# A decoder stack on one core: other PSUM banks for the attention layers, and masks ahead of the query projection

## The chip, the cores and the metric

The kernel runs on one core of one Trainium2 chip. The core has five engines that run side by side and meet through semaphores: TensorE (PE: matrix products and transposes, which write into PSUM), VectorE (DVE), ScalarE (ACT), GpSimd (POOL) and SyncE (SP, here for DMA). PSUM has 8 banks of 128 partitions by 512 fp32 values. Each engine takes its own instructions strictly in the order written; an instruction that waits holds up all behind it on the same engine. The metric is the device time of one execution in microseconds (us).

## The reference

Twelve layers of a decoder (four blocks of self attention, cross attention and feed forward) work on x of 8 sequences x 128 positions x 128 values, each as `x = x + layer(layernorm(x))`. Five of the twelve are attentions with 16 heads of 8 values: L0x (cross, rotary), L1a (self, causal), L1x (cross, with a distance bias), L2x (cross, with a mask), L3a (self, rotary, causal). L1x stands for them:

```
x = x + _L1_xattn_ref(_layernorm(x), ctx_1024, Wq, bq, Wkv, bkv, Wo, bo)

q = query @ Wq + bq
k, v = jnp.split(kv @ Wkv + bkv, 2, axis=-1)      # 16 heads of 8
scores = jnp.einsum('bhqd,bhkd->bhqk', q, k) * scale + bias[None]
attn = jax.nn.softmax(scores, axis=-1)
out = jnp.einsum('bhqk,bhkd->bhqd', attn, v)
return out @ Wo + bo
```

## The kernel before

**Two groups, woven.** The 8 sequences are two groups g = 0, 1 of four. For every engine one Python generator per group writes the instructions; each `yield n, phase` gives the layer's number and a phase, and `weave` (L83) always lets the generator with the smaller pair go on, group 0 where they are equal. So the order on every engine is fixed when the kernel is built, and the phases alone set it.

**Banks.** `bank(i)` of group g is PSUM bank 4g + i. In an attention layer the key projection goes to `bank(1)`, the value projection to `bank(2)`, the transposed layer norm to `bank(3)`, the query projection to `bank(0)` (in L0x and L3a banks 0 and 1 hold the rows first and later their transposes). ACT reads them into SBUF as `QT`, `KT` and `vaug` (L915 or L913, L865 or L823, L834); in L1x and L2x DVE writes `vaug` and adds its bias (L1148).

**Units.** A unit u is one half (8 heads) of one sequence's heads; a group has 8 units. Its scores take two banks. Three pairs of banks, `PAIRS` (L177), go round between the groups: unit u of group g uses pair (2u + g) mod 3. Banks 6 and 7 hold the weighted values of group 0 and 1. For a unit PE writes the mask into the two banks (`biased`, L441: an identity times a bf16 mask, one matmul a bank, in L1x three), adds the scores on top (`scores`, L453: two matmuls over 32 partitions), DVE takes the maximum (L1155) and subtracts it into SBUF (L1161), PE transposes the eight heads back into the same two banks (`turned`, L466, its instructions at L469), ACT takes the exponential (L843), and PE multiplies with the values (`weighted`, L472). POOL spreads the keys of one sequence over heads (`KTm`, L333; the first of L0x, L1a and L3a is DVE's, L1143).

**The opening.** `attend` of PE (L439) first waits, for both groups, for QT, KT and vaug, since unit 0 of group 0 lies in banks 4 and 5 and unit 0 of group 1 in banks 2 and 3. Then PE's order is: mask and scores of unit 0 of group 0, the same of group 1, transposes of unit 0 of group 0, mask and scores of its unit 1, and so on. In L1x and L2x the keys and values of both groups are projected at phase 0, xn is transposed at phase 2, q projected at phase 4, and `attend` begins at phase 20. In L1a q, k and v are projected at phase 4; in L0x and L3a queries and keys are rotated on DVE and POOL and transposed at phase 8.

**The end.** `out_proj` (L514) turns the result in `bank(2)` and projects it into `bank(0)`. As these belong to pairs in turn, it waits for the last exponential but one of group 1 (group 0) or for the last result of group 0 (group 1).

Of the kernel before, what the change touches and what calls it, by code (L numbers as in the profile page):

```python
# [14 lines left out]
P = 128  # L15
B = 8
GB = 4
GROUPS = B // GB
W4 = GB * P
H = 16  # L20
HD = P // H
HG = 4
# [69 lines left out]
def build(nc, x_d, ctx_d, mask_d, w_d, r_d, c_d, k_d, b_d, out_d, marks):  # L92
# [81 lines left out]
        return bank  # L174

    all_banks = ps[:, :].rearrange("p (b c) -> p b c", c=512)
    PAIRS = (all_banks[:, 4:6, :], all_banks[:, 2:4, :], all_banks[:, 0:2, :])  # L177

    def pair(g, u):

# [221 lines left out]
    def _(pe):  # L402
        def mm(out, lhsT, rhs, start=True, stop=True, **k):
            return pe.matmul(out, lhsT, rhs, start=start, stop=stop, **k)  # L404
# [11 lines left out]
        def program(g):  # L416
# [22 lines left out]
            def attend(n, l):  # L439

                def biased(u, i):  # L441

                    r, out = 2 * (u % 2) + i, pair(g, u)[:, i, :]
                    if l == "L1x":
                        odd = out.rearrange("p (j k) -> p j k", j=HG)[:, 1::2, :]
                        mm(out, identb, alibi0[:, HG * r:HG * r + HG, :], stop=False)
                        mm(odd, identb, alibi1[:, 2 * r:2 * r + 2, :], start=False, stop=False)
                        mm(odd, identb, alibi2[:, 2 * r:2 * r + 2, :], start=False, stop=False)
                    else:
                        mask = t.dmask[:, u // 2, :] if l == "L2x" else causalb  # L450
                        mm(out, identb, mask.unsqueeze(1).to_broadcast([P, HG, P]), stop=False)

                def scores(u):  # L453
                    b, half = divmod(u, 2)
                    if 2 * u + g >= 3:
                        pe.wait_ge(*s.at(f"{l}.exp{(2 * u + g - 3) // 2}", 1 - g))
                    for i in range(2):
                        biased(u, i)
                    if half == 0:
                        pe.wait_ge(*s.at(f"{l}.keys{b}"))  # L460
                    for i in range(2):
                        r = 32 * (2 * half + i)
                        ins = mm(pair(g, u)[:, i, :], QT[r:r + 32, b * P:(b + 1) * P], t.KTm[r:r + 32, b % 2, :, :], start=False, tile_position=(r, 0))
                    ins.then_inc(*s.step(f"S{u}"))

                def turned(u):  # L466
                    pe.wait_ge(*s.at(f"{l}.sub{u}"))
                    for j in range(HH):
                        ins = pe.transpose(heads_of(pair(g, u))[:, j // HG, j % HG, :], pr[:, (u % 2) * HH + j, :], ident)  # L469
                    ins.then_inc(*s.step(f"T{u}"))  # L470

                def weighted(u):  # L472

                    b, half = divmod(u, 2)
                    if half == 0 and b:
                        pe.wait_ge(*s.at(f"{l}.co{b - 1}"))
                    pe.wait_ge(*s.at(f"{l}.exp{u}"))
                    for j in range(HH):
                        h, at = HH * half + j, 32 * (j % HG)
                        ins = mm(all_banks[at:at + 32, 6 + g, h // HG * P:(h // HG + 1) * P], t.vaug[:, b, h, :], PT[:, (u % 2) * HH + j, :], tile_position=(0, at))  # L480
                    ins.then_inc(*s.step(f"O{u}"))

                def back(b):

                    pe.wait_ge(*s.at(f"{l}.OT{b}"))
                    for i in range(GB):
                        ins = pe.transpose(all_banks[:, 6 + g, i * P:(i + 1) * P], t.td[:, i, :], ident)  # L487
                    ins.then_inc(*s.step(f"OR{b}"))

                yield n, 20  # L490
                for other in (g, 1 - g):
                    pe.wait_ge(*s.at(f"{l}.QT", other))
                    pe.wait_ge(*s.at(f"{l}.KT", other))
                    pe.wait_ge(*s.at(f"{l}.vaug", other))
                if l == "L1x":
                    pe.wait_ge(loaded["alibi"], 16)
                if l == "L2x":
                    pe.wait_ge(*s.at("L0a.dmask"))
                scores(0)
                for u in range(UNITS):  # L500
                    yield n, beat(g, u, 2)
                    if u >= 3 and u % 2 == 1:
                        back(u // 2 - 1)
                    turned(u)
                    if u + 1 < UNITS:
                        scores(u + 1)
                    if u:
                        weighted(u - 1)
                yield n, beat(g, UNITS)
                weighted(UNITS - 1)  # L510
                yield n, beat(g, UNITS, 2)
                back(GB - 1)

            def out_proj(n, l, weight, turn=2, out=0):  # L514
                yield n, 130
                if l in SCALES:
                    pe.wait_ge(*(s.at(f"{l}.exp{UNITS - 2}", 1) if g == 0 else s.at(f"{l}.co{GB - 1}", 0)))
                pe.wait_ge(*s.at(f"{l}.co{GB - 1}"))
                turn_rows(turn, t.co, "coTp")
                yield n, 131  # L520
                pe.wait_ge(*s.at(f"{l}.coT"))
                project_rows(out, t.coT, weight, "y")

            def gates(bk, weight, n):
                for b in range(GB):
# [19 lines left out]
            for n, l in enumerate(LAYERS[1:STAGES + 1]):  # L545
# [43 lines left out]
                if l in ("L0x", "L3a"):  # L589
                    yield n, 4  # L590
                    pe.wait_ge(*s.at(f"{l}.xnT"))
                    project_rows(0, xnT, w(f"{l}_wq"), "q")
                    if l == "L3a":
                        project_rows(1, xnT, w("L3a_wk"), "k")
                        project_rows(2, xnT, w("L3a_wv"), "v")
                    yield n, 8
                    pe.wait_ge(*s.at(f"{l}.qrot"))
                    turn_rows(0, t.tc, "QTp")
                    pe.wait_ge(*s.at(f"{l}.krot"))
                    turn_rows(1, t.td, "KTp")  # L600
                    yield from attend(n, l)
                    yield from out_proj(n, l, w(f"{l}_wo"))
                if l in ("L1a", "L1x", "L2x"):
                    yield n, 4
                    pe.wait_ge(*s.at(f"{l}.xnT"))
                    project_cols(0, xnT, w(f"{l}_wq"), "q")
                    if l == "L1a":
                        project_cols(1, xnT, w("L1a_wk"), "k")
                        project_rows(2, xnT, w("L1a_wv"), "v")
                    yield from attend(n, l)  # L610
                    yield from out_proj(n, l, w(f"{l}_wo"))
                if l == "L0f":
# [197 lines left out]
    def _(act):  # L810
# [5 lines left out]
        def program(g):  # L816
# [19 lines left out]
            def attend(n, l):  # L836
                for u in range(UNITS):
                    yield n, beat(g, u, 4)
                    act.wait_ge(*s.at(f"{l}.T{u}"))
                    if u >= 2:  # L840
                        act.wait_ge(*s.at(f"{l}.O{u - 2}"))
                    half = PT[:, (u % 2) * HH:(u % 2 + 1) * HH, :].rearrange("p (i j) k -> p i j k", i=2)
                    act.activation(half, heads_of(pair(g, u)), ACT.Exp, scale=SCALES[l]).then_inc(*s.step(f"exp{u}"))  # L843
                    if u >= 2 and u % 2 == 0:
                        yield n, beat(g, u, 5)
                        weighted_out(u // 2 - 1, l)
                yield n, beat(g, UNITS, 1)
                weighted_out(GB - 1, l)
                yield n, 130
                read(t.coT[:, :], bank(2), "coTp", "coT")  # L850

            def weighted_out(b, l):
                if b:
                    act.wait_ge(*s.at(f"{l}.OR{b - 1}"))
                read(t.td[:, :, :], four(all_banks[:, 6 + g, :]), f"O{2 * b + 1}", f"OT{b}")

            for n, l in enumerate(LAYERS[1:STAGES + 1]):
                s.begin(l)
# [162 lines left out]
    def _(dve):  # L1021
# [48 lines left out]
        def program(g):  # L1070
# [60 lines left out]
            def attend(n, l):  # L1131
                def normal(b):
                    dve.wait_ge(*s.at(f"{l}.OR{b}"))
                    O = all_banks[:, 6 + g, :].rearrange("p (h d) -> p h d", h=H)
                    dve.reciprocal(t.rc[:, :], O[:, :, HD]).then_inc(*s.step())
                    dve.wait_ge(*s.last())
                    dve.tensor_tensor(t.co[:, b, :].rearrange("p (h d) -> p h d", h=H), O[:, :, 0:HD],
                                      wide(t.rc[:, :], HD), ALU.mult).then_inc(*s.step(f"co{b}"))
# [97 lines left out]
            for n, l in enumerate(LAYERS[1:STAGES + 1]):  # L1236
# [99 lines left out]
                    rotate(bank(0).rearrange("p (h d) -> p h d", d=HD), const("c3"), const("s3"), tc, "qrot", "pair")  # L1336
                if l in ("L0x", "L1a", "L1x", "L2x", "L3a"):
                    yield from attend(n, l)
                    yield from add(n, l, 0)
                if l == "L0f":  # L1340
                    yield from top2(n, l, E0, "bg0")
                    yield from mix(n, l, range(1, E0, 2), [e % 3 for e in range(E0)], lambda e: 21 + 4 * e)
# [303 lines left out]
```

## Time and profile before

| | us |
|---|---|
| median of 3 runs | 783.21 (782.43 to 784.71) |
| profiled execution, its own time | 782.54 |
| its span | 780.8 |
| PE busy (matmul) | 604.5 (77%) |
| PE busy (weight load, beside matmuls) | 393.9 (50%) |
| DVE busy | 497.1 (64%) |
| ACT busy | 243.5 (31%) |
| POOL busy | 118.6 (15%) |

The profile is of one execution. Times in its rows are counted from the start of the span. The chain that ended last is followed back from the last instruction, at each step to what released it or to the instruction before it on its engine. "Idle" in brackets is how long the engine did nothing before the row's first instruction, and what ended it; "issue" names no other engine. Neighbouring instructions of one line are merged in a row, with their count. The granted clock of PE is given as a share of 2.4 GHz: 1.00 is 2.4 GHz and 0.50 is 1.2 GHz.

### The profile page before, as it was taken

To read this page: it belongs to the slowest core of one execution; us is meant where nothing else is said; L and a number is where in the kernel's file an instruction comes from. 1 tells how busy PE (TensorE), PEld (TensorE's weight loads), DVE (VectorE), ACT (ScalarE), POOL (GpSimd) and SP (SyncE) were. 2 spreads that over 40 slices of the span, in tenths; PEclk is the share of its full clock that TensorE was granted. 3 is DMA by queue.
4 is the path that set the end of the run, shared out by engine and by line. 5 is a ranking of instruction groups with operands and counts; after the bars stand their busy time and mean duration, and the time that the engine had idled before them with its cause. 6 is when DMAs were issued, how large, how long until landed. Compare 5 with 4: busy or idle time off the path is not lost.

```text
span 780.8 us, 10935 instructions
## 1 busy us (share of the span) xinstructions
PE 604.5 (77%) x4305; PEld 393.9 (50%) x4305; DVE 497.1 (64%) x1338; ACT 243.5 (31%) x357; POOL 118.6 (15%) x118
## 2 busy tenths in 40 slices
PE   1306299977899789987997577899779968997376
PEld 1305145567455536665775545455535653565335
DVE  7777877667487647655244645786564355775694
ACT  0423124414244313333423331244221122343150
POOL 5021611014210212001002014110200043102110
PEclk9957579979899959997998798999789987999778
DMA  9600000000000000000000000000000000000000
GB/s 313 262 0 1 0 1 2 2 1 2 0 2 1 2 1 1 2 1 1 0 1 1 1 0 1 1 2 1 1 0 1 0 1 1 1 2 0 1 0 28
DMA packets 6722, 12.42 MB, mean 16 GB/s; under 512 B 528, under 2 KB 4880, under 8 KB 6288
## 3 DMA queue, kind: packets, MB, share of 16 engines
q1 hardware_dynamic: 6672, 11.73, 4.2%
q8 instruction: 34, 0.56, 0.3%
q14 instruction: 16, 0.13, 0.1%
HBM read 11.21 MB, written 0.52 MB: 15 GB/s over the span
## 4 chain that ended last, share of the span: by engine, by line
PE 68%; DVE 23%; ACT 4%; POOL 3%; issue 2%; DMA 1%; POOLq 0%; DVEq 0%; SPq 0%; ACTq 0%
PE ps L404 51%; PE ps L469 10%; PE ps L487 3%; DVE xn L1245 3%; PE ps L426 3%; DVE st L1077 2%; POOL rs L322 2%; DVE mx L1155 1%; DVE big L1161 1%; DVE x L1175 1%; DVE mv L1080 1%; DVE big L1087 1%; ACT td L823 1%; ACT big L843 1%; PE ps L676 1%
## 5 line engine op out<-in xcount | busy, mean ns | idle before, releaser
L1155 DVE TENSOR_REDUCE mx<-ps 128x8 f32<-128x1024 f32 x80 | 98.0, 1225 | 66.9 <-PE ps L404 66.8
L843 ACT ACTIVATE big<-ps 128x1024 f32<-128x1024 f32 x80 | 81.9, 1024 | 145.7 <-PE ps L469 145.7
L1161 DVE TENSOR_TENSOR big<-ps,mx 128x1024 f32<-128x1024 f32 x80 | 97.7, 1222 | 4.7 <-DVE mx L1155 0.5
L404 PE MATMUL ps<-KTm,qk 32*128 32x512 f32 x320 | 96.5, 680 | 0.0
L322 POOL TENSOR_TENSOR rs<-ve,negh 128x4 f32<-128x4 f32 x26 | 26.6, 1024 | 420.6 <-DVE ve L1082 420.5
L469 PE MATMUL ps<-kt,big 128*128 128x128 f32 x640 | 88.4, 283 | 2.3 <-DVE big L1161 2.0
L404 PE MATMUL ps<-xnT,wt 128*128 128x512 f32 (+1 forms) x148 | 84.1, 711 | 3.1 <-DVE big L1400 3.1
L469 PEld LDWEIGHTS ps<-kt,big 128*128 128x128 f32 x640 | 71.9, 144 | 23.5 <-DVE big L1161 12.5
L404 PE MATMUL ps<-wt,big 128*128 128x128 f32 (+1 forms) x480 | 61.0, 280 | 0.0
L404 PEld LDWEIGHTS ps<-wt,big 128*128 128x128 f32 (+1 forms) x480 | 56.4, 191 | 8.0 <-issue 6.0
L333 POOL TENSOR_TENSOR KTm<-qk,kt 128x512 f32<-128x512 f32 x34 | 37.5, 1111 | 117.4 <-PE ps L404 108.9
L404 PEld LDWEIGHTS ps<-big,vaug 128*32 128x32 f32 x1280 | 30.4, 109 | 48.0 <-ACT big L843 30.3
L404 PE MATMUL ps<-bt 128*128 128x512 bf16 (+1 forms) x192 | 50.1, 374 | 3.6 <-ACT qk L823 1.8
L426 PE MATMUL ps<-kt,xn 128*128 128x128 f32 x80 | 18.3, 373 | 43.7 <-DVE xn L1245 43.5
L404 PE MATMUL ps<-big,vaug 128*32 128x128 f32 x1280 | 50.5, 278 | 0.0
L404 PEld LDWEIGHTS ps<-xnT,wt 128*128 128x128 f32 (+1 forms) x148 | 30.9, 226 | 34.9 <-issue 28.3
L404 PEld LDWEIGHTS ps<-KTm,qk 32*128 32x128 f32 x320 | 25.5, 195 | 33.4 <-issue 33.4
L1221 DVE SCALAR_TENSOR_TENSOR x<-ps,gw,x 128x128 f32<-128x128 f32 x80 | 22.2, 344 | 31.5 <-PE ps L404 30.8
L404 PEld LDWEIGHTS ps<-wt,xnT 128*128 128x128 f32 x256 | 37.8, 235 | 3.6 <-issue 3.0
L823 ACT ACTIVATE td<-ps 128x512 f32<-128x512 f32 x42 | 25.1, 598 | 43.3 <-PE ps L404 42.9
L404 PE MATMUL ps<-wt,xnT 128*128 128x128 f32 (+2 forms) x256 | 37.9, 310 | 0.2 <-ACT xnT L823 0.2
L426 PEld LDWEIGHTS ps<-kt,xn 128*128 128x128 f32 x80 | 11.9, 185 | 48.2 <-issue 31.1
(252 smaller groups left out, 797.5 us busy)
## 6 DMA issues: line engine op xcount, KB each, us to landing
wt<-in_weights SPq DMA_DIRECT2D x1, 1664.0 KB, 17.8
wt<-in_weights SPq DMA_DIRECT2D x1, 1603.0 KB, 12.5
wt<-in_weights SPq DMA_DIRECT2D x6, 256.0 KB, 11.7
bt<-in_bconsts SPq DMA_DIRECT2D x1, 1024.0 KB, 8.9
rowt<-in_rows SPq DMA_DIRECT2D x1, 975.0 KB, 5.9
wt<-in_weights SPq DMA_DIRECT2D x1, 832.0 KB, 14.1
wt<-in_weights SPq DMA_DIRECT2D x1, 608.0 KB, 19.2
wt<-in_weights SPq DMA_DIRECT2D x1, 580.0 KB, 5.8
```

What stands on the lines that cost most here:

```text
L322: pool.tensor_tensor(out, src, negh[:, :], ALU.pow).then_inc(*s.step(name + "_r"))
L333: pool.tensor_tensor(t.KTm[:, b % 2, :, :], keys_of(t, b), own_head(), ALU.mult).then_inc(*s.step(f"keys{b}"))
L404: return pe.matmul(out, lhsT, rhs, start=start, stop=stop, **k)
L426: ins = pe.transpose(seq(bk, b), src[:, b, :], ident)
L469: ins = pe.transpose(heads_of(pair(g, u))[:, j // HG, j % HG, :], pr[:, (u % 2) * HH + j, :], ident)
L487: ins = pe.transpose(all_banks[:, 6 + g, i * P:(i + 1) * P], t.td[:, i, :], ident)
L823: act.activation(out, src, ACT.Copy).then_inc(*s.step(name))
L843: act.activation(half, heads_of(pair(g, u)), ACT.Exp, scale=SCALES[l]).then_inc(*s.step(f"exp{u}"))
L1155: dve.tensor_reduce(top, S, AX.X, ALU.max).then_inc(*s.step())
L1161: dve.tensor_tensor(pr[:, half * HH:(half + 1) * HH, :].rearrange("p (i j) k -> p i j k", i=2), S, top.unsqueeze(3).to_broadcast([P, 2, HG ...
L1221: dve.scalar_tensor_tensor(x[:, b, :], bank(banks[e])[:, b * P:(b + 1) * P], gw[:, b, e:e + 1], x[:, b, :], ALU.mult, ALU.add).then_inc(*s ...
L1245: dve.tensor_scalar(xn[:, b, :], x[:, b, :], t.mv[:, b, 0:1], t.rs[:, b:b + 1], ALU.subtract, ALU.mult).then_inc(*s.step("xn"))
```

## The change

The three pairs become banks 1-2, 5-6 and 3-4, and the weighted values move to bank 0 (group 0) and bank 7 (group 1), named `VALUES`. Unit 0 of each group then lies in that group's own key and value banks. The mask part of `scores` becomes a function of its own, `masked`. `attend` waits for the group's own keys and values only, writes the first mask, and in L1x and L2x issues the query projection after that mask; then it waits for the group's own queries ahead of the first scores. Unit 1 of group 0 waits for group 1's queries, unit 1 of group 1 for the exponential as before. `out_proj` turns in `bank(0)` and projects into `bank(3)` for group 0, and `bank(3)` and `bank(0)` for group 1, and its two waits on the other group go. DVE and ACT follow with the bank names alone.

```diff
--- before.py
+++ after.py
@@ -174,7 +174,8 @@
         return bank
 
     all_banks = ps[:, :].rearrange("p (b c) -> p b c", c=512)
-    PAIRS = (all_banks[:, 4:6, :], all_banks[:, 2:4, :], all_banks[:, 0:2, :])
+    PAIRS = (all_banks[:, 1:3, :], all_banks[:, 5:7, :], all_banks[:, 3:5, :])
+    VALUES = tuple(all_banks[:, k, :] for k in (0, 7))
 
     def pair(g, u):
 
@@ -450,12 +451,16 @@
                         mask = t.dmask[:, u // 2, :] if l == "L2x" else causalb
                         mm(out, identb, mask.unsqueeze(1).to_broadcast([P, HG, P]), stop=False)
 
+                def masked(u):
+                    if 2 * u + g >= 3:
+                        pe.wait_ge(*s.at(f"{l}.exp{(2 * u + g - 3) // 2}", 1 - g))
+                    elif u:
+                        pe.wait_ge(*s.at(f"{l}.QT", 1))
+                    for i in range(2):
+                        biased(u, i)
+
                 def scores(u):
                     b, half = divmod(u, 2)
-                    if 2 * u + g >= 3:
-                        pe.wait_ge(*s.at(f"{l}.exp{(2 * u + g - 3) // 2}", 1 - g))
-                    for i in range(2):
-                        biased(u, i)
                     if half == 0:
                         pe.wait_ge(*s.at(f"{l}.keys{b}"))
                     for i in range(2):
@@ -477,25 +482,29 @@
                     pe.wait_ge(*s.at(f"{l}.exp{u}"))
                     for j in range(HH):
                         h, at = HH * half + j, 32 * (j % HG)
-                        ins = mm(all_banks[at:at + 32, 6 + g, h // HG * P:(h // HG + 1) * P], t.vaug[:, b, h, :], PT[:, (u % 2) * HH + j, :], tile_position=(0, at))
+                        ins = mm(VALUES[g][at:at + 32, h // HG * P:(h // HG + 1) * P], t.vaug[:, b, h, :], PT[:, (u % 2) * HH + j, :], tile_position=(0, at))
                     ins.then_inc(*s.step(f"O{u}"))
 
                 def back(b):
 
                     pe.wait_ge(*s.at(f"{l}.OT{b}"))
                     for i in range(GB):
-                        ins = pe.transpose(all_banks[:, 6 + g, i * P:(i + 1) * P], t.td[:, i, :], ident)
+                        ins = pe.transpose(VALUES[g][:, i * P:(i + 1) * P], t.td[:, i, :], ident)
                     ins.then_inc(*s.step(f"OR{b}"))
 
-                yield n, 20
-                for other in (g, 1 - g):
-                    pe.wait_ge(*s.at(f"{l}.QT", other))
-                    pe.wait_ge(*s.at(f"{l}.KT", other))
-                    pe.wait_ge(*s.at(f"{l}.vaug", other))
+                pe.wait_ge(*s.at(f"{l}.KT"))
+                pe.wait_ge(*s.at(f"{l}.vaug"))
                 if l == "L1x":
                     pe.wait_ge(loaded["alibi"], 16)
                 if l == "L2x":
                     pe.wait_ge(*s.at("L0a.dmask"))
+                masked(0)
+                if l in ("L1x", "L2x"):
+                    yield n, 4
+                    pe.wait_ge(*s.at(f"{l}.xnT"))
+                    project_cols(0, xnT, w(f"{l}_wq"), "q")
+                yield n, 20
+                pe.wait_ge(*s.at(f"{l}.QT"))
                 scores(0)
                 for u in range(UNITS):
                     yield n, beat(g, u, 2)
@@ -503,6 +512,7 @@
                         back(u // 2 - 1)
                     turned(u)
                     if u + 1 < UNITS:
+                        masked(u + 1)
                         scores(u + 1)
                     if u:
                         weighted(u - 1)
@@ -511,15 +521,13 @@
                 yield n, beat(g, UNITS, 2)
                 back(GB - 1)
 
-            def out_proj(n, l, weight, turn=2, out=0):
+            def out_proj(n, l, weight):
                 yield n, 130
-                if l in SCALES:
-                    pe.wait_ge(*(s.at(f"{l}.exp{UNITS - 2}", 1) if g == 0 else s.at(f"{l}.co{GB - 1}", 0)))
                 pe.wait_ge(*s.at(f"{l}.co{GB - 1}"))
-                turn_rows(turn, t.co, "coTp")
+                turn_rows(3 * g, t.co, "coTp")
                 yield n, 131
                 pe.wait_ge(*s.at(f"{l}.coT"))
-                project_rows(out, t.coT, weight, "y")
+                project_rows(3 - 3 * g, t.coT, weight, "y")
 
             def gates(bk, weight, n):
                 for b in range(GB):
@@ -598,15 +606,19 @@
                     turn_rows(0, t.tc, "QTp")
                     pe.wait_ge(*s.at(f"{l}.krot"))
                     turn_rows(1, t.td, "KTp")
+                    yield n, 20
                     yield from attend(n, l)
                     yield from out_proj(n, l, w(f"{l}_wo"))
+                if l == "L1a":
+                    yield n, 4
+                    pe.wait_ge(*s.at("L1a.xnT"))
+                    project_cols(0, xnT, w("L1a_wq"), "q")
+                    project_cols(1, xnT, w("L1a_wk"), "k")
+                    project_rows(2, xnT, w("L1a_wv"), "v")
+                    yield n, 20
+                if l in ("L1x", "L2x"):
+                    yield n, 3
                 if l in ("L1a", "L1x", "L2x"):
-                    yield n, 4
-                    pe.wait_ge(*s.at(f"{l}.xnT"))
-                    project_cols(0, xnT, w(f"{l}_wq"), "q")
-                    if l == "L1a":
-                        project_cols(1, xnT, w("L1a_wk"), "k")
-                        project_rows(2, xnT, w("L1a_wv"), "v")
                     yield from attend(n, l)
                     yield from out_proj(n, l, w(f"{l}_wo"))
                 if l == "L0f":
@@ -847,12 +859,12 @@
                 yield n, beat(g, UNITS, 1)
                 weighted_out(GB - 1, l)
                 yield n, 130
-                read(t.coT[:, :], bank(2), "coTp", "coT")
+                read(t.coT[:, :], bank(3 * g), "coTp", "coT")
 
             def weighted_out(b, l):
                 if b:
                     act.wait_ge(*s.at(f"{l}.OR{b - 1}"))
-                read(t.td[:, :, :], four(all_banks[:, 6 + g, :]), f"O{2 * b + 1}", f"OT{b}")
+                read(t.td[:, :, :], four(VALUES[g]), f"O{2 * b + 1}", f"OT{b}")
 
             for n, l in enumerate(LAYERS[1:STAGES + 1]):
                 s.begin(l)
@@ -1131,7 +1143,7 @@
             def attend(n, l):
                 def normal(b):
                     dve.wait_ge(*s.at(f"{l}.OR{b}"))
-                    O = all_banks[:, 6 + g, :].rearrange("p (h d) -> p h d", h=H)
+                    O = VALUES[g].rearrange("p (h d) -> p h d", h=H)
                     dve.reciprocal(t.rc[:, :], O[:, :, HD]).then_inc(*s.step())
                     dve.wait_ge(*s.last())
                     dve.tensor_tensor(t.co[:, b, :].rearrange("p (h d) -> p h d", h=H), O[:, :, 0:HD],
@@ -1336,7 +1348,7 @@
                     rotate(bank(0).rearrange("p (h d) -> p h d", d=HD), const("c3"), const("s3"), tc, "qrot", "pair")
                 if l in ("L0x", "L1a", "L1x", "L2x", "L3a"):
                     yield from attend(n, l)
-                    yield from add(n, l, 0)
+                    yield from add(n, l, 3 - 3 * g)
                 if l == "L0f":
                     yield from top2(n, l, E0, "bg0")
                     yield from mix(n, l, range(1, E0, 2), [e % 3 for e in range(E0)], lambda e: 21 + 4 * e)
```

## Rows read from the trace of the kernel before

**Rows 1.** The page: the span, and the shares by engine of the chain that ended last.

```profile
span 780.8 us, 10935 instructions
...
PE 68%; DVE 23%; ACT 4%; POOL 3%; issue 2%; DMA 1%; POOLq 0%; DVEq 0%; SPq 0%; ACTq 0%
```

**Rows 2.** The chain in order of time, middle of L1a: start, duration, what.

```profile
217.39 2.06 PE ps L404 x22
220.47 2.06 PE ps L404 x22
```

**Rows 3.** Timeline, opening of L0x: start, duration, instruction, count, [idle before <-releaser].

```profile
95.42 1.12 PE L426 MATMUL ps<-kt,td 128*128 128x128 f32 x4
...
97.42 1.01 PE L404 MATMUL ps<-bt 128*128 128x512 bf16 x2 [0.88 <-ACT qk L823]
...
98.36 2.08 PE L404 MATMUL ps<-KTm,qk 32*128 32x512 f32 x4
...
101.75 1.22 DVE L1161 TENSOR_TENSOR big<-ps,mx 128x1024 f32<-128x1024 f32 x1
...
103.35 1.97 PE L469 MATMUL ps<-kt,big 128*128 128x128 f32 x8
```

**Rows 4.** Timeline, opening of L1a.

```profile
205.06 1.05 PE L404 MATMUL ps<-wt,xnT 128*128 128x128 f32 x8
...
206.89 0.59 PE L404 MATMUL ps<-bt 128*128 128x512 bf16 x2 [0.78 <-ACT vaug L834]
```

**Rows 5.** Timeline, opening of L3a.

```profile
645.87 0.77 PE L426 MATMUL ps<-kt,td 128*128 128x128 f32 x4 [3.52 <-POOL td L357]
...
647.53 1.01 PE L404 MATMUL ps<-bt 128*128 128x512 bf16 x2 [0.88 <-ACT qk L823]
```

**Rows 6.** Timeline, opening of L1x, to the third set of transposes.

```profile
274.90 1.66 DVE L1148 TENSOR_TENSOR vaug<-ps,rowt 128x128 f32<-128x128 f32 x8
...
275.04 1.12 PE L426 MATMUL ps<-kt,xn 128*128 128x128 f32 x4 [3.52 <-DVE xn L1245]
...
275.95 3.62 PE L404 MATMUL ps<-xnT,wt 128*128 128x512 f32 x4
...
280.61 1.87 PE L404 MATMUL ps<-bt 128*128 128x512 bf16 x6 [1.04 <-issue]
...
282.40 2.08 PE L404 MATMUL ps<-KTm,qk 32*128 32x512 f32 x4
...
284.53 1.23 DVE L1155 TENSOR_REDUCE mx<-ps 128x8 f32<-128x1024 f32 x1 [7.96 <-PE ps L404]
...
288.24 1.97 PE L469 MATMUL ps<-kt,big 128*128 128x128 f32 x8
...
292.66 1.10 PE L469 MATMUL ps<-kt,big 128*128 128x128 f32 x8
...
295.61 1.09 PE L469 MATMUL ps<-kt,big 128*128 128x128 f32 x8
```

**Rows 7.** Timeline, opening of L2x.

```profile
484.10 1.12 PE L426 MATMUL ps<-kt,xn 128*128 128x128 f32 x4 [3.52 <-DVE xn L1245]
...
489.67 0.59 PE L404 MATMUL ps<-dmask,bt 128*128 128x512 bf16 x2 [1.04 <-issue]
...
490.19 1.13 PE L404 MATMUL ps<-KTm,qk 32*128 32x512 f32 x4
...
491.36 1.23 DVE L1155 TENSOR_REDUCE mx<-ps 128x8 f32<-128x1024 f32 x1 [5.74 <-PE ps L404]
```

**Rows 8.** Windows, PE: stretch, length, busy (instructions), granted clock, DMA share, GB/s.

```profile
106.00:107.00 1.00, 1.00 (x3) 0.52 0.00 0
...
202.00:203.00 1.00, 1.00 (x6) 0.73 0.00 0
...
291.00:292.00 1.00, 1.00 (x6) 0.86 0.00 0
...
489.00:490.00 1.00, 0.33 (x2) 0.87 0.00 0
```

## The prediction

> **What bounds the kernel now.** I read the page first: of the 780.8 us span, the chain that ended last lies 68% on TensorE (PE) and 23% on VectorE (DVE) [rows 1]. Then I read the chain in order of time inside one attention layer. In its steady part the same 22 matmuls come round with nothing of another engine between them, 3.08 us apart [rows 2]. So the middle of an attention layer is a PE queue that never runs dry. The change leaves that queue as it is, matmul for matmul; only bank numbers differ. What it can move is the opening of the five attention layers (L0x, L1a, L1x, L2x, L3a): how soon the first scores of group 0 are there, and at which clock. Layers follow each other strictly, so what an opening gains stays to the end. For that I read the timeline of each opening, with the idle time that it prints before an instruction and who ended it [rows 3 to 7], and last the granted clock [rows 8].
>
> **Opening of L0x, L1a and L3a.** Before, both groups' queries, keys and values must be read out of PSUM before group 0's first mask matmul, for its unit writes banks 4 and 5, which belong to group 1. After, it writes banks 1 and 2, its own keys and values, and waits for these alone. They have long been read in all three layers, so the first mask follows right behind the last PE instruction ahead of it.
> - L0x: group 1's key transposes start at 95.42 and take 1.12, so they end at 96.54; the mask starts at 97.42, after 0.88 of idle that a ScalarE (ACT) read ended [rows 3]. Gain 0.88. Does what follows come along? Transposes of unit 0 started at 103.35, when PE was free; DVE's subtraction, which they need, was done at 101.75 + 1.22 = 102.97. PE was the later, by 0.38, and both move by 0.88.
> - L1a: group 1's value projection starts at 205.06 and takes 1.05, so it ends at 206.11; the mask starts at 206.89, idle 0.78 until ACT had the values [rows 4]. Gain 0.78.
> - L3a: transposes 645.87 + 0.77 end at 646.64, mask at 647.53 after 0.88 idle [rows 5]. Gain 0.88.
>
> The wait that is late next is group 1's own read: its mask comes only behind group 0's mask (0.94 at half clock, start to start [rows 3]) and scores (about 2), later than the 0.88 that the reads need. Group 0's unit 1 now waits for group 1's queries; it stands a whole unit later. Sum of the three: 2.54 us.
>
> **Opening of L1x and L2x.** Here masks also move ahead of the query projections. PE's order was: transpose xn of group 0, of group 1, project q of 0, of 1, [wait], masks 0, scores 0, masks 1, scores 1, transposes 0. It becomes: transposes of xn, masks 0, masks 1, q 0, q 1, scores 0, scores 1, transposes 0. The new wait stands on PE ahead of both projections, with all the queries behind it, ACT's reads and the scores. It asks for the values: eight DVE additions from 274.90 on, done at 276.56, the first four at about 275.7. PE ends its transposes at 276.16, so group 0 has some 0.4 to spare and group 1, a mask set later, 1.4 [rows 6]. It costs nothing; were DVE 1 us later, 0.6 would come on top. The long idle of PE before 275.04 (3.52, waiting for xn) is not filled, since the masks stand behind that transpose. What goes is the 1.04 of idle between q of group 1 and masks 0.
>
> L1x with the clock at half throughout, as in this execution: masks cost 1.79 a group (280.61 to 282.40), the two projections 3.41 (276.16 to 279.57). 276.16 + 3.58 + 3.41 = 283.15 for the first score instead of 282.40, so DVE's maximum, 2.13 after it, starts at 285.28 instead of 284.53. PE is ahead now (free at 283.15 + 2 x 2.02 = 287.2) and DVE is late next: 285.28 + 2.5 (maximum and subtraction, 1.23 each and a hand-over, [rows 3, 6]) = 287.8 for transposes 0 against 288.24. Gain 0.4.
>
> L1x with a better clock: the record shows that PE worked at 1.2 GHz from 275.04 until the clock rose in the slice 291.00 to 292.00, 16 us, with 4.5 us of transposes and projections, the idle 1.04, and then masks and scores. In L1a it rose in 202.00 to 203.00, after transposes and projections without a gap from about 196.9, so 5.7 us; in L2x in 489.00 to 490.00, 5 us after 484.10; in L0x only at the end of 106.00 to 107.00, after a start like L1x's: short, a gap, then masks and scores [rows 3, 4, 6, 7, 8]. After the change L1x has 276.16 - 275.04 + 3.58 + 3.41 = 8.1 us of transposes, masks and projections without a gap, longer than L1a's 5.7. If it rises at 280.7, the 2.45 us left of these halve: first score at 281.9, maximum at 283.1 (a full-clock pair of scores and hand-over being 1.17 [rows 7]), subtracted at 285.6, transposes 0 at 285.6, and one unit step at full (2.95, from 292.66 to 295.61) brings transposes of group 1 to 288.6 against 292.66 [rows 6]. Gain 4.1.
>
> So the ends are 0.4 and 4.1. I take 1.5. The reason against the upper end is L2x: the same instructions in the same order, with the same 1.04 gap, had the clock back before the masks, in this same execution [rows 7, 8]. Where L1x does the same before the change, nothing is left to gain by the clock (the two mask sets then lie ahead of q at half speed, about what the idle was). I count the slow opening as the rarer of the two.
>
> The Trainium skill bears on this: "TensorE: Matmul & The Clock Gate", Part 1: The HAM clock gate, says that how many matmuls run cold at a start differs from run to run of the same kernel, 6, 11 or 14 in one case. The openings of L1x and L2x in this trace agree, 16 and 5 us for the same order. By that rule the 4.1 is not a property of the two kernels but partly of this execution; by the trace alone it would be booked in full and the sum would be 6.8.
>
> L2x: transposes end at 485.22. Two masks are two matmuls a group, at half 1.01, so 487.24; projections 3.41 at half would end at 490.65, but the clock was up from about 489.3, which leaves 489.95. Maximum 1.17 later, 491.12, against 491.36: gain 0.24 [rows 3, 7, 8]. Bounds: with the clock up later the first score is at 490.65 instead of 490.19 and scores are 2.02 instead of 1.06, a loss of 1.4; with full clock all through, the 1.04 idle less one group's masks (0.52), a gain of 0.5. I take 0.2.
>
> **Clock in L0x and L3a.** Both open at half, PE-bound. Starting 0.88 sooner may put one unit step more at half, or fewer. The trace of before can't show which. A step costs 4.42 at half (288.24 to 292.66) and 2.95 at full [rows 6], so 1.5 either way in each; I take 0 and keep the bound.
>
> **The end of the layers.** The output projection changes banks (0 and 3 for group 0, 7 and 4 for group 1) and loses two waits. Nothing is gained: on PE group 0's turn stands behind group 1's last turn back of outputs, which is later than either event waited for. Value buffers move to banks 0 and 7, whose last readers (queries, xn) are done before the first scores. Instruction and DMA counts stay.
>
> **Sum.** 2.54 + 1.5 + 0.2 = 4.24. The profiled execution took 782.54 (span 780.8 and 1.7 around it): 778.3. The runs' median, 783.21, is 0.67 above it, so 779.0 is what I predict.
>
> **Rivals.**
> - The gap goes and nothing else (25%): 2.54, with L1x at 0.4 and L2x at its loss of 1.4 or its 0.2: 1.5 to 3.1 in all, so about 780.5. For it: L2x shows that the clock may have been back without the change. Against it: rows 4 and 6 side by side.
> - The clock gain is there in full (14%): 2.54 + 4.1 + 0.2 = 6.8, so 776.4 by the median, 774.9 if one half-clock step goes in L0x too. For it, the 8.1 us without a gap; against it, L2x.
> - The change does not do what it says (10%): the openings start sooner but the units are held by another link, such as keys on GpSimd or DVE's two reads a unit, and the time comes out at 782.5 to 783.5. For it: DVE's pair is late next in L1x. Against it: the 3.08 period holds only PE work [rows 2].
> - Slower (6%): group 0's masks and scores start sooner and fill the stretch ahead of the clock's rise, and L1a and L2x, which open at full now, open at half as L1x did. Price: 3.7 each (4.1 less 0.4) and 1.5 for a step in L0x, 8.9, less 2.9: 6 us over, 789. It decides when the clock in L1a and L2x has not risen before the first maximum; one of them alone gives about 784.
>
> **Numbers.** Forecast 45%, the others as given. Range: it leaves out most of the slower case and the far end of the full clock gain: 775.6 to 782.6. About 0.3% (2.35 us) is what a measurement of this kernel can tell from no change, so the line is at 780.9: forecast and clock gain lie beyond it (59%) and over half of the first rival (14%): faster 0.73. Same: 0.21. Slower: 0.06.
>
> **What would show it.** The first mask of L0x, L1a and L3a with under 0.15 idle before it; in L1x and L2x masks ahead of the projections and no 1.04 gap; in L1x a clock that is up by about 282 on the old time base, and the first maximum 1.4 sooner rather than 0.75 later. Wrong: an idle of PE before the masks in L1x (values late); a 3.08 period that has grown; the clock at half for longer in L1a or L2x than it was.

## The result and the profile after

The changed kernel takes 771.13 us in the median of four executions (770.15 to 772.77), the one before 783.86 (782.43 to 784.71): a ratio of 0.984, 95% interval 0.982 to 0.987. A second set of five gave 770.66 and again 0.984 (0.982 to 0.986). It is 12.7 us faster; 4.2 were forecast, and the time lies below the stated range.

The page of the profiled execution (772.77 us, the slowest of its four): span, shares of the chain, granted clock in 40 slices.

```profile
span 771.0 us, 10907 instructions
...
PEclk9956569979899989997998898999799987999778
...
PE 67%; DVE 22%; ACT 3%; POOL 3%; issue 2%; DMA 1%; SPq 0%; POOLq 0%; DVEq 0%; ACTq 0%
```

The chain's shares stand within one point of [rows 1], though the span is 9.8 us shorter. The first question is whether the gaps at the openings went. The chain in order of time (start, duration, what), opening of L0x and then of L3a:

```profile
95.65 1.11 PE ps L427 x4
96.77 5.83 PE ps L405 x12
102.60 1.90 PE ps L474 x8
...
637.28 1.12 PE ps L427 x4
638.39 5.83 PE ps L405 x12
```

The masks now follow the transposes at once; the 0.88 of idle in [rows 3] and [rows 5] is gone, and L0x's first transposes of a unit are at 102.53 in the timeline instead of 103.35, although this execution came to L0x's key transposes 0.23 later (95.65 against 95.42). L1a, L1x and L2x in the timeline:

```profile
205.80 1.05 PE L405 MATMUL ps<-wt,xnT 128*128 128x128 f32 x8
...
206.69 0.59 PE L405 MATMUL ps<-bt 128*128 128x512 bf16 x2
...
274.78 1.12 PE L427 MATMUL ps<-kt,xn 128*128 128x128 f32 x4 [3.52 <-DVE xn L1257]
276.11 2.63 PE L405 MATMUL ps<-bt 128*128 128x256 bf16 x11 [0.22 <-DVE vaug L1160]
278.58 1.88 PE L405 MATMUL ps<-xnT,wt 128*128 128x512 f32 x4
280.39 1.99 PE L405 MATMUL ps<-KTm,qk 32*128 32x512 f32 x8
...
284.10 1.30 PE L474 MATMUL ps<-kt,big 128*128 128x128 f32 x8 [1.73 <-DVE big L1173]
...
477.81 1.12 PE L427 MATMUL ps<-kt,xn 128*128 128x128 f32 x4 [3.52 <-DVE xn L1257]
478.72 1.91 PE L405 MATMUL ps<-dmask,bt 128*128 128x512 bf16 x4
480.43 3.08 PE L405 MATMUL ps<-xnT,wt 128*128 128x512 f32 x4
483.43 1.99 PE L405 MATMUL ps<-KTm,qk 32*128 32x512 f32 x8
```

The order is the one foretold, the 1.04 of [rows 6, 7] is gone, and the new wait for the values costs 0.22, where the prediction had put nothing. In L1x the clock came back during the masks, so that the two pairs of scores took 1.99 together where before they took 2.08 each. Now DVE is late (1.73 of idle on PE). DVE's first maximum and PE's second set of transposes, from the same timeline:

```profile
281.56 1.22 DVE L1167 TENSOR_REDUCE mx<-ps 128x8 f32<-128x1024 f32 x1 [5.26 <-PE ps L405]
...
288.68 1.09 PE L474 MATMUL ps<-kt,big 128*128 128x128 f32 x8
```

The maximum is 3.0 earlier than in [rows 6], the second set of transposes 4.0. The clock around these places (window, length, busy, granted clock):

```profile
110.00:111.00 1.00, 1.00 (x5) 0.62 0.00 0
202.00:203.00 1.00, 1.00 (x2) 0.54 0.00 0
274.00:275.00 1.00, 0.22 (x1) 0.80 0.00 0
278.00:279.00 1.00, 1.00 (x7) 0.99 0.00 0
284.00:285.00 1.00, 0.90 (x8) 0.92 0.00 0
288.00:289.00 1.00, 1.00 (x7) 0.87 0.00 0
```

A slice of 1.00 us with a mean of 0.80 was at full for 0.60 of it (the levels are 0.50 and 1.00), so in L1x the clock fell at 274.6 and rose at 278.0, against 291.3 before [rows 8]. It also fell once more for 3.4 us from 284.8, while PE worked on transposes, after the 1.73 of idle; that is why 4.58 lie between the first transposes (284.10) and the second, where a step at full clock is 2.95. In L0x it rose at 110.8, 3.8 later than in [rows 8]. In L1a it rose at 202.9, 7.3 into the layer (which began at 195.62), against 202.5 and 8.0 before.

Layer by layer (from one group 0 rsqrt of the layer norm on GpSimd, L322 before and L323 after, to the next; my subtraction), us in the profiled executions:

| layer | before | changed | difference |
|---|---|---|---|
| up to L0x | 68.06 | 68.12 | +0.06 |
| L0x | 94.47 | 95.57 | +1.10 |
| L0f | 32.00 | 31.93 | -0.07 |
| L1a | 74.08 | 72.73 | -1.35 |
| L1x | 84.55 | 80.77 | -3.78 |
| L1f | 58.88 | 57.69 | -1.19 |
| L2a | 65.63 | 64.58 | -1.05 |
| L2x | 73.70 | 73.16 | -0.54 |
| L2f | 76.55 | 75.15 | -1.40 |
| L3a | 84.44 | 83.07 | -1.37 |
| L3x, L3f | 68.44 | 68.23 | -0.21 |

Of the 9.8 us, 5.9 lie in the five attention layers, and 3.9 in layers whose instructions nobody changed. The other 2.9 of the 12.7 are between these two executions and the medians: the traced one of before lies 1.3 below its median, the changed one 1.6 above. A second trace of the changed kernel (772.57) has the same times of layers within 0.7. All nine executions of the two sets fall into two groups: four at 772.1 to 772.8, with a mean granted clock of 0.884, to which both traces belong, and five at 770.2 to 770.7, with 0.886 or 0.906.

### The profile page after: what moved, and what is told of

The parts are those of the page before. It is cut to its first block, busy times and chain, and to the rows that moved or that the text cites. A ratio compares the mean times of both kernels' runs of the same rounds, so it can differ in the third digit from the quotient of the medians.

```text
span 771.0 us, 10907 instructions
## 1 busy us (share of the span) xinstructions
PE 597.1 (77%) x4297; PEld 392.5 (51%) x4305; DVE 496.8 (64%) x1338; ACT 243.4 (32%) x357; POOL 118.8 (15%) x118
## 4 chain that ended last, share of the span: by engine, by line
PE 67%; DVE 22%; ACT 3%; POOL 3%; issue 2%; DMA 1%; SPq 0%; POOLq 0%; DVEq 0%; ACTq 0%
PE ps L405 51%; PE ps L474 10%; PE ps L492 3%; PE ps L427 2%; DVE xn L1257 2%; DVE st L1089 2%; POOL rs L323 1%; DMA bt<-in_bconsts 1%; DVE mx L1167 1%; DVE big L1173 1%; DVE x L1187 1%; DVE mv L1092 1%; ACT td L835 1%; ACT big L855 1%; DVE big L1365 1%
## 5 line engine op out<-in xcount | busy, mean ns | idle before, releaser
L323 POOL TENSOR_TENSOR rs<-ve,negh 128x4 f32<-128x4 f32 x26 | 26.6, 1024 | 415.7 <-DVE ve L1094 415.6
L474 PEld LDWEIGHTS ps<-kt,big 128*128 128x128 f32 x640 | 71.9, 144 | 26.2 <-DVE big L1173 14.9
L405 PE MATMUL ps<-xnT,wt 128*128 128x512 f32 (+1 forms) x148 | 78.4, 669 | 3.1 <-DVE big L1412 3.1
L405 PE MATMUL ps<-bt 128*128 128x512 bf16 (+1 forms) x184 | 48.1, 373 | 0.6 <-DVE vaug L1160 0.2
```

The lines of the kernel that those rows point to most:

```text
L323: pool.tensor_tensor(out, src, negh[:, :], ALU.pow).then_inc(*s.step(name + "_r"))
```

## The experiments

Each run is compared with the kernel before on the same chip (783.5, 783.4 and 782.9 in the three sets, 16 to 23 executions each). "Layer times" are taken as in the table, each from the one traced execution of its run. The runs switch lines by tuples of layer names; the edits of the first two are shown with these conditions worked out, so that they read as what the kernel does, and so is the shift's call of `fill`.

**Does the layout itself save anything?** The changed kernel with the old waits and order:

```diff
+                if l in ("L1x", "L2x"):
+                    yield n, 4
+                    pe.wait_ge(*s.at(f"{l}.xnT"))
+                    project_cols(0, xnT, w(f"{l}_wq"), "q")
+                    yield n, 20
                 pe.wait_ge(*s.at(f"{l}.KT"))
                 pe.wait_ge(*s.at(f"{l}.vaug"))
+                for other in (g, 1 - g):
+                    pe.wait_ge(*s.at(f"{l}.QT", other))
+                    pe.wait_ge(*s.at(f"{l}.KT", other))
+                    pe.wait_ge(*s.at(f"{l}.vaug", other))
...
                 masked(0)
-                if l in ("L1x", "L2x"):
-                    yield n, 4
-                    pe.wait_ge(*s.at(f"{l}.xnT"))
-                    project_cols(0, xnT, w(f"{l}_wq"), "q")
```

> The new banks alone: the first mask of every attention layer waits for both groups' queries, keys and values as before, and stands behind the query projections. Theory 1 (the time comes from the gaps of PE at the openings and from the clock that follows them): no gap closes, so the time of the kernel before, 783 to 785, with the same clock in L1x (at half until about 291). Rival (the bank numbers themselves, or the two waits dropped at the end of the layers, save time): 775 or less.

784.0 (781.9 to 785.4), ratio 1.001 (1.000 to 1.002). The banks and the two waits dropped in `out_proj` are worth nothing that shows. Layer by layer its profile lies within 0.2 us of the one before: L1x again took 84.6 with the clock at half until 291.

**Is it the place of the masks?** The changed kernel, projections first in L1x and L2x, each group waiting for itself alone:

```diff
+                if l in ("L1x", "L2x"):
+                    yield n, 4
+                    pe.wait_ge(*s.at(f"{l}.xnT"))
+                    project_cols(0, xnT, w(f"{l}_wq"), "q")
+                    yield n, 20
                 pe.wait_ge(*s.at(f"{l}.KT"))
                 pe.wait_ge(*s.at(f"{l}.vaug"))
...
                 masked(0)
-                if l in ("L1x", "L2x"):
-                    yield n, 4
-                    pe.wait_ge(*s.at(f"{l}.xnT"))
-                    project_cols(0, xnT, w(f"{l}_wq"), "q")
```

> The changed kernel, but in L1x and L2x the masks stay behind the query projections; the first mask waits for its own group alone. Theory 1: the gaps close all the same, 0.88, 0.78 and 0.88 in L0x, L1a, L3a and the 1.04 in L1x and L2x, filled by group 0's masks, so about 771 as the changed kernel, perhaps 1 less, since group 1's masks no longer hold up group 0's scores. Rival (it is the place of the masks ahead of the projections that brings the clock back in L1x): 775 to 777, with L1x at half for long.

774.05 (770.1 to 775.4), ratio 0.988 (0.985 to 0.990). So most of the gain does not need the masks ahead. The gap is closed here by group 0's masks, and the scores come sooner still. The timeline of L1x in this run:

```profile
272.93 3.25 PE L405 MATMUL ps<-xnT,wt 128*128 128x512 f32 x4
276.23 0.82 PE L405 MATMUL ps<-bt 128*128 128x256 bf16 x5
276.98 1.13 PE L405 MATMUL ps<-KTm,qk 32*128 32x512 f32 x4
```

L1x took 78.4 against the changed kernel's 80.8; what the run lost lies elsewhere (L3a 85.3, L1f and L2a about 1.3 each above the changed kernel's). So neither the 771 that was expected nor the rival's 775 to 777 came. The medians are 3 us apart, but the intervals of the two ratios overlap (0.985 to 0.990, and 0.982 to 0.987), and the spans of the two traced executions are 770.9 and 771.0. That the order matters at this clock is likely, not shown, and which layers would lose by it stays open.

**One layer at a time.** The first of these kernels, with the new waits (and in L1x and L2x the new order) for the layers named alone; beside the tuple that stands here there are ("L0x",), ("L1a", "L3a") and ("L2x",):

```diff
+                if l not in ("L1x",):
                     for other in (g, 1 - g):
                         pe.wait_ge(*s.at(f"{l}.QT", other))
...
```

> The new banks everywhere, but own waits and early masks in L1x alone. Theory 1: L1x gains 3.8 as in the profile of the changed kernel, and the layers behind it start 3.8 sooner: 779 to 780 if these layers keep their own times. Rival (the layers behind it change their time with the moment at which they start): off that by 1 us or more, either way.

779.9 (776.5 to 782.0), ratio 0.995 (0.993 to 0.997), as expected. L1x: 80.35, a gain of 4.2 in its profile.

> New banks, own waits in L0x alone. Gap alone: 0.88 less, 782.6. Gap and clock: turns and masks now follow each other for 3.2 us instead of 2.2 and 1.0 with a gap between, and in part of the executions the clock is up before the first scores, as in one profile: 3 us less on the middle, 780 to 781, and a wide spread. Rival (the clock's rise only comes later, as in the profile of the changed kernel): 784.

777.7, ratio 0.993 (0.990 to 0.996), six executions at 773.4 to 775.0 and six at 780.3 to 782.2. The median is below the 780 to 781 expected. The low ones lie 8 to 10 below the kernel before, though the gap was 0.88.

> New banks, own waits in L1a and L3a alone. Gaps alone: 0.78 + 0.88, 781.8. With a clock gain as in L1x: 780 or less. If the parts add up to the whole 12.4 with 3.6 for L1x and 1 for L2x, L0x and these two must bring some 8 together, so below 780.

775.7 (774.7 to 777.8), ratio 0.990 (0.988 to 0.992): 7.6 less for 1.66 of gaps.

> New banks, own waits and early masks in L2x alone. My sum for L2x was a gain of 0.2, between a loss of 1.4 and a gain of 0.5: 783.3. If the closed gap brings the clock as in L1x: 780 to 781. Rival (masks at half speed ahead of the projections cost what the gap was): 783.5 to 784.5.

785.4, ratio 1.001 (0.999 to 1.003), two executions at 778 and ten at 783.7 to 787.8. Neither the forecast nor either rival named this. Its profile shows L2x 0.5 faster, L2f 1.3 faster and L3a 2.3 slower (86.7), with L0x 97.4 besides, where this kernel waits as before: with its old waits L0x took 94.5 to 97.6 in eight profiles.

The parts add up to 3.6 + 5.7 + 7.6 - 2.0 = 14.9, against 12.7 for the whole. With intervals of 1.4 to 2.2 us either way on each part, that difference alone shows nothing. What shows that the parts aren't independent is in the profiles of the L0x run and of the L1a and L3a run: L1x, whose waits and order neither changes, took 79.4 and 79.6 in them instead of 84.6. So three of the four parts hold the same 4 to 5 us of L1x. The windows of L1x in the L0x run, fall and rise:

```profile
273.00:274.00 1.00, 0.00 (x0) 0.77 0.00 0
276.00:277.00 1.00, 1.00 (x3) 0.52 0.00 0
```

The clock fell at 273.5 and was up at 277.0, with a gap between projections and masks (1.41 here) still there:

```profile
274.22 1.11 PE L427 MATMUL ps<-kt,xn 128*128 128x128 f32 x4 [3.52 <-DVE xn L1267]
275.12 2.80 PE L405 MATMUL ps<-xnT,wt 128*128 128x512 f32 x4
279.33 0.81 PE L405 MATMUL ps<-bt 128*128 128x256 bf16 x5 [1.41 <-ACT qk L937]
```

**The closed gap by itself.** The kernel before, with one matmul that nobody reads in L1x's gap:

```diff
+                    if l == "L1x" and g == 1:
+                        mm(bank(3)[:, 0:256], w("L1x_wq"), xnT[:, 0:256])
                     yield from attend(n, l)
```

> The kernel before, with one matmul more that nobody reads, 256 columns, on PE behind group 1's query projection in L1x: 0.85 us at half clock in the idle 1.04, nothing else moved. If the gap in PE's work kept the clock at half there: the clock is up before the first scores, and 3 to 4 us go in L1x, 779.5 to 781. If the clock gain came from starting sooner and not from the closed gap: 783 to 785.

780.4 (775.5 to 781.5), ratio 0.995 (0.993 to 0.997); L1x 80.1. Useless work alone, with no step made earlier, brings the 3 us, three times the 1.04 of idle. All nine executions lie below the lowest of the kernel before in this set (781.8). In the traced one 0.40 of idle was left, and L1x took 4.4 less than in the kernel before; but its clock fell 5.1 us into the layer and not at 5.6, so not all of the 4.4 need be the matmul's.

**A later start by itself.** The kernel before, with matmuls that nobody reads at the end of L1a, where PE is busy and at full clock (3 of them, then 8):

```diff
+                if l == "L1a" and g == 0:
+                    for _ in range(3):
+                        mm(bank(1)[:, 0:256], ident, kt[:, 0:256])
                 project_rows(out, t.coT, weight, "y")
```

> The kernel before with three matmuls more that nobody reads (128x256 fp32, about 0.43 us each at full clock) on PE at the end of L1a, where PE is busy and at full clock: everything from L1x on starts 1.3 us later, nothing else changes. Theory (what L1x costs depends on when the clock falls within its idle, and the kernel before always meets it at the same unlucky place, 84.5 us, while 1 to 2 us earlier or later it takes 79.5 to 80.5): faster than before in spite of the added work, 779.5 to 781.5. Rival (L1x gained by its closed gap alone; starting later only costs): 784.6.

780.1 (778.1 to 782.3), ratio 0.996 (0.995 to 0.998): faster by 2.8 for 1.3 us of added work. L1a took 75.4 (+1.3), L1x 80.1 (-4.4).

> The same with eight matmuls, 3.4 us. Theory: the clock meets L1x at the unlucky place again, so the added work is paid in full: 786 to 787.5, six more than with 1.3 us. Rival (a later start only costs): 786.8 too, but then the run with 1.3 us is at 784.6.

786.8 (785.0 to 788.5), ratio 1.005 (1.004 to 1.007): L1a 77.5 (+3.4), L1x 84.6 (0.0). In both shift runs every layer behind L1x took what it took before, within 0.1. The fall and rise in L1x, first in the run with 1.3 us, then with 3.4:

```profile
274.00:275.00 1.00, 0.00 (x0) 0.52 0.00 0
...
280.00:281.00 1.00, 0.56 (x1) 0.57 0.00 0
```

```profile
277.00:278.00 1.00, 0.00 (x0) 0.77 0.00 0
...
294.00:295.00 1.00, 1.00 (x7) 0.69 0.00 0
```

Seven profiles have L1x in its old form. When the clock fell, counted from the layer's first rsqrt, and what the layer took:

| run | fall | rise | L1x |
|---|---|---|---|
| before + 1.3 us | 4.43 | 11.3 | 80.1 |
| new in L2x only | 5.29 | 22.4 | 84.4 |
| before | 5.61 | 22.7 | 84.6 |
| before + 3.4 us | 5.65 | 22.7 | 84.6 |
| banks only | 5.69 | 22.8 | 84.6 |
| new in L0x only | 5.75 | 9.2 | 79.4 |
| new in L1a, L3a only | 6.15 | 9.6 | 79.6 |

The same instructions take 84.5 or 79.5 to 80, and which of the two goes with where the clock falls in the layer's idle: five cases of seven lie within half a microsecond (5.29 to 5.75), slow up to 5.69 and fast at 5.75; 6.15 is fast, and so is the early fall at 4.43. One profile each is thin for so fine a line.

One pair has the fall at the same place and differs in L1x's form alone up to the layer's end: new in L1x only, and new in L2x only, whose L1x is old. Their windows, L1x new and then L1x old:

```profile
277.00:278.00 1.00, 0.00 (x0) 0.51 0.00 0
283.00:284.00 1.00, 1.00 (x2) 0.57 0.00 0
```

```profile
276.00:277.00 1.00, 0.00 (x0) 0.57 0.00 0
293.00:294.00 1.00, 1.00 (x8) 0.89 0.00 0
```

The fall is 5.3 us into the layer in both. The new form has the clock back at 12.1 and takes 80.4; the old has it back at 22.4 and takes 84.4. So the new opening brings L1x's 4 us by itself too, where the place of the fall lends no help.

**Most of the half-speed time taken out.** Matmuls that nobody reads in the long idle stretches of PE, in the changed kernel and in the one with projections first. `FILLS` names 9 to 12 for the starts of L0f, L1a, L1f, L2a, L2f and L3a; further calls of `fill` stand in L0a (20), L0x (20 and 16), L2a (12 and 8), L3a (2 and 7) and L3f (14); the ones at the start of L1a and the 12 in L2a have a wait of their own, so that they fall into the idle:

```diff
+            def fill(k, out):
+                for _ in range(k):
+                    mm(out[:, 0:256], ident, kt[:, 0:256])
...
+                if g == 1 and l in FILLS:
+                    fill(FILLS[l][0], bank(FILLS[l][1]))
                 if l not in ("L0a", "L3f"):
                     yield n, 2
                     pe.wait_ge(*s.at(f"{l}.xn"))
                     turn_rows(3, xn, "xnTp")
+                    if g == 0 and l in ("L1x", "L2x"):
+                        fill(7, bank(0))
```

> The changed kernel with matmuls that nobody reads (identity x constants, 128x256 fp32) in the long idle stretches of PE: in L0a, in L0x and L3a before and between the transposes of queries and keys, at the start of L0f, L1a, L1f, L2a, L2f and L3a, twice inside L2a, between the two transposes of xn in L1x and L2x, and at the start of L3f; each run of them shorter than the idle was. Theory (what is left between kernels of this family is the clock): PE at half for 182 us of 771 now; most of that goes, and with it 20 to 35 us: 735 to 750, with a small spread. Rival (the clock matters only in the openings of attention; elsewhere other engines bound): 765 or more.

751.2 (750.6 to 754.8), ratio 0.960 (0.959 to 0.962), a little above the 735 to 750 that were expected.

> The same fillers in the variant with the query projections ahead of the masks in L1x and L2x. At full clock the first scores need not wait for both groups' masks: some 0.9 sooner in L1x and 0.5 in L2x, so 1 to 1.5 less than the other filled kernel. Rival (the order of masks and projections is worth nothing at full clock): the same.

750.5 (749.0 to 754.0), ratio 0.959 (0.957 to 0.961): within 1 us of the other, so the 1 to 1.5 expected for the order of masks and projections does not show at a clock that is mostly up. The page of this run:

```profile
span 749.1 us, 11587 instructions
...
PEclk9986999999999999998999999999889999999878
```

By the mean granted clock (0.954 here, 0.884 in the changed kernel) the half-speed time is 69 us of 749 instead of 179 of 771, and each filled kernel is about 20 us faster than the changed one.

## Why the prediction was wrong

Two steps failed, and both are about the clock: the 1.5 taken for L1x, and the step that put nothing on the layers behind an opening. By the profiles, forecast and measured (4.24 and 9.8) part as follows: layers with unchanged instructions +3.9, L1x +2.3, L1a and L3a beyond their gaps +1.1, L2x +0.3, L0x -2.0, together 5.6. Another 2.9 lie between the profiles and the medians.

- **The missing term, the largest.** "What an opening gains stays to the end", with nothing added by the layers behind, and no reason given for that nothing. In the profiles, 3.9 of 9.8 us lie in layers with unchanged instructions: L1f, L2a and L2f each took 1.1 to 1.4 less, and in L1f the clock came back 2.4 us earlier, counted from the layer's start (356.1 to 366.4 at half in a layer that began at 353.2, against 349.7 to 359.9 in one that began at 349.1). In the one-layer runs it is plainer still: 0.88 of gap in L0x brought 5.7 in the median, and L1x, a later layer, took 5 us less in that profile. The shift runs show the mechanism in one layer (L1x); for L1f, L2a and L2f it is inferred from the same profiles and was not isolated. A sooner start is not enough for it: in the run with 1.3 us L1x also ended some 3 us sooner, and L1f, L2a and L2f took what they took before.
- **L1x, the term that was mis-sized.** Its two ends were 0.4 and 4.1, 1.5 was taken, and the measured 3.8 to 4.2 is the upper end. The words for 1.5 were "I count the slow opening as the rarer of the two", from L2x in the same trace and a rule that starts differ from run to run. The runs show otherwise: the kernel before stayed within 781.5 to 785.5 in all executions of four sets; four profiles of its old L1x (before, banks only, new in L2x only, and 3.4 us added) had the clock at half until 22 to 23 us into the layer; and a filled gap took 3 us off the median. As far as these runs go, the slow opening was the rule for this kernel, and 1.3 us of added work, or an L0x or L1a that ends sooner, was what took it away. The Trainium skill's sentence ("TensorE: Matmul & The Clock Gate", Part 1: The HAM clock gate) that cold starts vary from run to run is borne out by L0x in its old form, where the clock rose in the slice 106 to 107 before [rows 8] and 5 us later in the run with L2x alone (a layer of 94.5 and of 97.4). I stretched it to mean that L1x meets the good and the bad case alike, which it does not.
- **The upper end of L1x hit by luck.** 4.1 was worked out with the clock back at 280.7, the first maximum 1.4 sooner, and a step of 2.95 behind it. In the trace the clock was back at 278.0 and the maximum came 3.0 sooner, and then a second fall made that step 4.58. The two errors nearly cancel.
- **The gaps (2.54 us).** Right in mechanism: the idle of 0.88, 0.78 and 0.88 is gone, and PE's next work moved up with it. L3a's layer time fell by 1.37 and L1a's by 1.35, more than the gap in each; L0x's rose by 1.10, since its clock came back 3.8 us later. That was the "one unit step more at half", bounded at 1.5 and taken at 0. Where the clock is kinder, the same L0x took 93.0 (with projections first) and 93.2 (changed by itself).
- **L2x.** Forecast a gain of 0.2; 0.54 in the profile, the upper bound. By itself the edit is worth nothing in the median (785.4); in its profile L3a took 2.3 more.
- **The values' wait and the end of the layers.** The wait was put at nothing and cost 0.22 of idle; an idle there was one of the signs named for "wrong", but it is small against the rest. Nothing for `out_proj` was right.
- **Rivals.** "The clock gain is there in full" (14%, 776.4) was the nearest, and still 5 too high. "The gap goes and nothing else" and "does not do what it says" are out: the openings moved, and so did the clock. "Slower" named a true mechanism, seen in L0x, at a price that never came together.

What stays open: what the executions without a trace do differently, and so why the whole is 12.7 and its profile 9.8. Those at 770 may hold L0x's fast form (the low half of the L0x run is 7 us below its high half), but no trace of one was taken.

## What to carry to other kernels

Price a gap on PE by two numbers: its length, and what the granted clock does in the 10 to 20 us behind it. Here the second was three times the first or more (3.1 us in the median for a filled 1.04, 5.7 for a closed 0.88), and in the run with 1.3 us of added work it decided the sign. A small shift can redraw one later layer and leave the rest: 1.3 us took 4.4 off L1x, 3.4 us took nothing off it, and the layers behind it stayed the same in both. So gains of single edits that all reach the same layer can't be added up, and a single profile per variant can't carry a clock term; test with a pure shift, or compare two profiles in which the clock falls at the same place. Where PE idles a few us again and again, try filling the idle before tuning the order: it gave 20 us on top of the 13 of the whole change (in the kernel before it was not tried).

## What the runs showed of the hardware

- The clock can fall while PE works: in the changed kernel at 284.8, in the middle of transposes, 0.7 us after an idle of 1.73 that followed scores over 32 partitions; it stayed at half for 3.4 us.
- Half speed can outlast 10 us of unbroken matmuls: before, from 280.6 to 291.3 in L1x, with masks and scores over 32 partitions and then transposes [rows 6, 8].
- Adding 1.3 us of work made the kernel 2.8 us faster, and 3.4 us made it 3.9 slower.
- Matmuls that nobody reads, put into PE's idle, gave back more than they cost: 680 instructions more and about 20 us less than the changed kernel.
